# A vision-tower kernel on one Trainium2 core: variance of the last two images from row sums and squares, and the last attention, turns, counts and placings in another order

## What is computed

```python
h = tok_ref(x, scharr)                       # grey image, 2 edge filters, |.|, summed, /2
h = layernorm(h + attn(h, Wq, bq, Wk, bk, Wv, bv))
h = layernorm(h + ffn(h, Wr, W1, W2))

def layernorm(x, eps=1e-5):
    return (x - mean(x)) / sqrt(var(x) + eps)

# ffn: each token goes to its best expert, if it is among that expert's first 320
probs = softmax(t @ Wr); idx = argmax(probs); pmax = max(probs)
pos   = position of the token among those of its expert (a running count)
ein   = tokens of each expert; h = relu(ein @ W1); eout = h @ W2
out   = where(pos < 320, eout * pmax, t)
```

## Time and profile before

| | |
|---|---|
| median of 3 runs | 245.89 us (245.63 to 246.35) |
| the profiled execution | 245.8 us, of it a span of 244.1 us in the trace |
| PE busy | 230.0 us, 94% |
| DVE busy | 185.3 us, 76% |
| ACT busy | 152.2 us, 62% |
| POOL busy | 96.6 us, 40% |
| stage one, stretch between, stage two | to about 100 us, 100 to 110.5 us, 110.5 to 234.7 us (last matmul), then the last rows |

### The profile page before, as it was taken

How to read it: one execution, slowest core, us unless ns; L and a number is a source line. 1 busy time by engine, 2 the same in 40 slices (tenths; PEclk the granted TensorE clock), 3 DMA queues, 4 the chain that set the end, 5 groups by cost and what they waited for, 6 DMA issues and landing times.

```text
span 244.1 us, 5000 instructions
## 1 busy us (share of the span) xinstructions
PE 230.0 (94%) x1670; PEld 222.3 (91%) x1670; DVE 185.3 (76%) x558; ACT 152.2 (62%) x355; POOL 96.6 (40%) x170
## 2 busy tenths in 40 slices
PE   6999999999999999889999999999999999999940
PEld 5999999999999998658999999999999999999940
DVE  6878797787979798897676767967779677789550
ACT  5336567786877887466675676674766757666100
POOL 7001228474665656557000025232262322623672
PEclk9999999999999999999999999999999999999995
DMA  5925975083796020301899919064090650100100
GB/s 169 299 74 178 284 234 151 26 237 151 238 394 228 6 83 3 85 0 50 245 352 361 349 48 359 3 214 167 12 379 10 201 176 3 48 0 24 36 4 0
DMA packets 28666, 35.88 MB, mean 147 GB/s; under 512 B 2684, under 2 KB 25579, under 8 KB 28642
## 3 DMA queue, kind: packets, MB, share of 16 engines
q1 hardware_dynamic: 26434, 32.11, 40.8%
q0 software_dynamic: 1792, 3.47, 3.9%
q10 hardware_dynamic: 416, 0.00, 0.1%
HBM read 27.37 MB, written 9.47 MB: 151 GB/s over the span
## 4 chain that ended last, share of the span: by engine, by line
PE 85%; issue 4%; POOL 4%; DVE 3%; ACT 2%; POOLq 1%; DMA 0%; ACTq 0%; DVEq 0%
PE bank L1329 16%; PE bank L1330 15%; PE bank L1331 15%; PE bank L1400 14%; PE bank L1417 5%; PE bank L1454 5%; POOL out_dram L589 3%; PE bank L1586 2%; PE bank L1470 2%; PE bank L1636 2%; PE bank L1494 2%; PE bank L1428 2%; PE bank L1472 1%; PE bank L1471 1%; POOL yrstd L613 1%
## 5 line engine op out<-in xcount | busy, mean ns | idle before, releaser
L1243 DVE SCALAR_TENSOR_TENSOR h_lo<-bank,h_hi 128x320 fp32r<-128x320 f32 x58 | 28.3, 490 | 24.7 <-ACT h_hi L854 21.9
L854 ACT ACTIVATE h_hi<-bank 128x320 fp32r<-128x320 f32 x58 | 25.4, 438 | 34.6 <-PE bank L1331 34.6
L1329 PE MATMUL bank<-einT_hi,w_hi 128*128 128x320 f32 x128 | 40.3, 315 | 0.2 <-DVE einT_lo L1235 0.2
L1331 PE MATMUL bank<-einT_hi,w_lo 128*128 128x320 f32 x128 | 39.6, 309 | 0.0
L1330 PE MATMUL bank<-einT_lo,w_hi 128*128 128x320 f32 x128 | 39.5, 309 | 0.0
L589 POOL DMA_INDIRECT out_dram<-tokens_mem,images x24 | 27.7, 1155 | 29.3 <-ACT tokens_mem L871 22.2
L992 DVE TENSOR_TENSOR w_lo<-w_raw,w_hi 128x1024 fp32r<-128x1024 f32 x32 | 38.9, 1216 | 0.0
L1329 PE MATMUL bank<-h_hi,w_hi 128*128 128x320 f32 x112 | 35.1, 313 | 0.0
L1330 PE MATMUL bank<-h_lo,w_hi 128*128 128x320 f32 x112 | 34.6, 309 | 0.0
L1331 PE MATMUL bank<-h_hi,w_lo 128*128 128x320 f32 x112 | 34.6, 309 | 0.0
L771 ACT ACTIVATE w_hi<-w_raw 128x1024 fp32r<-128x1024 f32 x32 | 33.7, 1054 | 0.0
(11 more groups left out here) (235 smaller groups left out, 570.9 us busy)
## 6 DMA issues: line engine op xcount, KB each, us to landing
w_raw<-in_L_ffn_W_dram SPq DMA_DIRECT2D x16, 1024.0 KB, 8.0
images<-in_x_dram SPq DMA_DIRECT2D x7, 768.0 KB, 5.1
dispatched<-blank SPq DMA_DIRECT2D x4, 645.0 KB, 9.6
images<-dispatched SPq DMA_DIRECT2D x6, 387.0 KB, 9.2
out_dram<-lone SPq DMA_DIRECT2D x8, 256.0 KB, 7.7
images<-dispatched SPq DMA_DIRECT2D x3, 258.0 KB, 4.4
images<-in_x_dram SPq DMA_DIRECT2D x2, 384.0 KB, 5.3
out_dram<-tokens_mem,images POOLq DMA_INDIRECT x24, 3.5
```

Source lines behind the costliest of these rows:

```text
L854: act.activation(hidden_halves(n)[0], hidden_bank(n)[:, 0:CAP], ACT.Relu).then_inc(h_hi_ready, 1)
L1243: dve.scalar_tensor_tensor(lo, hidden_bank(n)[:, 0:CAP], 0.0, hi.bitcast(F32), ALU.max, ALU.subtract).then_inc(h_ready, 1)
L1329: pe.matmul(to, ah, bh, start=first, stop=False)
L1331: return pe.matmul(to, al, bh, start=False, stop=last)
```

## The change

For images 6 and 7 (L - 1 and L) the statistics are no longer made by bn_stats and bn_aggr. The residual sum on DVE also gives the row's sum (`accum_out`), DVE makes the negative mean of it (`row_mean`), ACT squares the residual with that as its bias and sums it (`square_rows`), and POOL makes variance, epsilon and power. The rows of image 6 are normalised by DVE (`norm_late_rows`) rather than by ACT; of image 7 the lower half is normalised by ACT (`norm_last_rows`) and the upper half by DVE.

The lists of the stretch are reordered. On PE `keep_warm(4)` is gone; `early_turn` is cut in two, one part for each chunk, and the first part stands between `late_prob_t` and `late_attend`, the second between the turn of the upper block and its product; the lower half's two products are swapped; three placings of image 6 stand ahead of `count(7)` and one behind; image 7 is placed with the lower half first. On DVE the bias of the upper half comes after `compare(6)`, the reciprocals, the gate sums and the means are cut by halves and stand beside the half that they belong to, and `number(6)` comes before the residual. On ACT the squares of image 6 stand before the first probabilities, `late_values(0)` after `late_prob_t`. `lsub` has two buffers.

```diff
@@ vector: the list of the last two images @@
             keys_low(L)
+            row_mean(L - 1, slice(0, SC), SC * L)
             residual_in(L, 0)
             residual_in(L, 1)
             softmax_max(L)
-            moments(L - 1)
             compare(L - 1)
-            softmax_sum(L)
+            late_bias(1, 0)
+            late_sum(0, 1)
+            for s in range(SC):
+                norm_late_rows(L - 1, s, L)
             add_places(L - 1)
-            late_residual()
-            moments(L)
+            number(L - 1)
+            late_residual(0, 1)
+            late_gate(1)
+            row_mean(L, slice(1, 2), SC * L + 1)
+            late_sum(1, 0)
+            late_residual(1, 0)
+            late_gate(0)
+            row_mean(L, slice(0, 1), SC * L + 2)
             route(L)
             factor(L - 1)
-            number(L - 1)
             compare(L)
+            norm_late_rows(L, 0, L + SC)
             add_places(L)
@@ vector: new functions @@
+            def row_mean(b, s, residuals):
+                dve.wait_ge(resid_ready, residuals)
+                dve.tensor_scalar(row_nmean[:, b % 2, s], row_sum[:, b % 2, s], -1.0 / D, None, ALU.mult
+                                  ).then_inc(row_mean_ready, 1)
+            def norm_late_rows(b, s, scales):
+                dve.wait_ge(rstd_ready, scales)
+                dve.wait_ge(rows_out[b % TR], 16 * SC * (b // TR))
+                dve.tensor_scalar(trow[:, b % TR, s, 0:D], resid[:, b % 2, s, :], row_nmean[:, b % 2, s:s + 1],
+                                  rstd[:, b % 2, s:s + 1], ALU.add, ALU.mult).then_inc(late_t_ready, 1)
@@ scalar @@
+            def square_rows(b, s, means):
+                act.wait_ge(pT_done, b + 1)
+                act.wait_ge(row_mean_ready, means)
+                act.activation(prob[:, s, :], resid[:, b % 2, s, :], ACT.Square, bias=row_nmean[:, b % 2, s:s + 1],
+                               accum_out=row_square[:, b % 2, s:s + 1]).then_inc(row_square_ready, 1)
...
             late_values(1)
+            for s in range(SC):
+                square_rows(L - 1, s, 1)
+            act.wait_ge(row_square_ready, SC)
+            late_probs(0, 1)
             late_constant(0)
-            late_probs(0, 1)
+            late_prob_t()
             late_values(0)
-            late_prob_t()
             late_probs(1, 0)
             late_prob_t_top()
-            norm_rows(L - 1)
             route_exp(L - 1)
-            norm_rows(L)
+            square_rows(L, 1, 2)
+            square_rows(L, 0, 3)
+            norm_last_rows()
             route_exp(L)
@@ gpsimd @@
+            def scale_square(b, s, squares):
+                pool.wait_ge(row_square_ready, squares)
+                link(pool.tensor_scalar(ve[:, s], row_square[:, b % 2, s], 1.0 / D, EPS, ALU.mult, ALU.add))
+            def scale_last_rows():
+                b = L
...
+                for n, s in enumerate((slice(1, 2), slice(0, 1))):
+                    scale_square(b, s, SC + n + 1)
+                    ins = pool.tensor_tensor(rstd[:, b % 2, s], ve[:, s], minus_half[:, s], ALU.pow)
+                    if n == 0:
+                        link(ins)
+                        ins = pool.tensor_tensor(nmr[:, b % 2, s], row_nmean[:, b % 2, s], rstd[:, b % 2, s], ALU.mult)
+                    ins.then_inc(rstd_ready, 1)
@@ tensor @@
-            keep_warm(4)
...
+            def early_turn(c):
+                pe.wait_ge(rowc_ready, L + SC - c)
+                pe.wait_ge(late_values_ready, SC - c)
                 pe.wait_ge(ein_in[0], 32)
                 pe.wait_ge(spare_rows_ready, 1)
...
-            early_turn()
-            place(L - 1)
+            late_prob_t()
+            early_turn(1)
+            late_attend()
+            late_prob_t_top()
+            early_turn(0)
+            late_attend_top()
+            place(L - 1, 1, 0)
+            place(L - 1, 1, 1)
+            place(L - 1, 0, 0)
             count(L)
-            place(L)
+            place(L - 1, 0, 1)
+            for c in range(DC):
+                for s in (1, 0):
+                    place(L, c, s)
```

More of the change, by code:

```diff
@@ L743, in norm_lone @@
                 act.wait_ge(lone_scale_ready, b + 1)
[L744 removed]
+                act.wait_ge(t_ready, SC * (b + 1) if b < L - 1 else SC * (L - 1) + (b - L + 1))
+                if b >= L - 1:
+                    act.wait_ge(late_t_ready, SC + b - L + 1)
                 if b >= 2:
@@ L759, in route_exp @@
                 for s in range(SC):
-                    ins = act.activation(lexp[:, s, :], lsub[:, s, :], ACT.Exp, scale=rstd[:, b % 2, s:s + 1],
+                    ins = act.activation(lexp[:, s, :], lsub[:, b % 2, s, :], ACT.Exp, scale=rstd[:, b % 2, s:s + 1],
                                          accum_out=lsum[:, s:s + 1])
@@ L1127, in compare @@
                 if b >= L - 1:
-                    for s in range(SC):
+                    for s in range(SC) if b < L else (1, 0):
                         dve.tensor_scalar(pick(b, s), slot_index, mine[:, b % 2, s, 0:1], None, ALU.is_equal
@@ L1548, in late_attend @@
                           ).then_inc(attn_done, 1)
-            late_prob_t()
-            late_attend()
-            def place(b):
-                for c in range(DC):
-                    for s in range(SC):
-                        pe.wait_ge(pick_ready, SC * (b - L + 1) + s + 1)
-                        pe.wait_ge(t_ready, SC * b + s + 1)
-                        ins = pe.matmul(bank[c][:, 0:CAP], trow[:, b % TR, s, c * P:(c + 1) * P], pick(b, s),
-                                        start=False, stop=(b == L and s == SC - 1),
-                                        skip_group_check=True)
-                    if b == L:
-                        ins.then_inc(einT_done, 1)
@@ L1565, in early_turn @@
-            def early_turn():
-                pe.wait_ge(rowc_ready, B + 1)
-                pe.wait_ge(late_values_ready, SC)
+            def early_turn(c):
+                pe.wait_ge(rowc_ready, L + SC - c)
+                pe.wait_ge(late_values_ready, SC - c)
                 pe.wait_ge(ein_in[0], 32)
                 pe.wait_ge(spare_rows_ready, 1)
-                for c in range(DC):
-                    for j, (o, _) in enumerate(SLOTS):
-                        ins = pe.matmul(bank[c][:, o:o + P], ein[:, 0, j, c * P:(c + 1) * P], ident[:, :],
-                                        start=(j == 0), stop=False, is_transpose=True, skip_group_check=True)
+                for j, (o, _) in enumerate(SLOTS):
+                    ins = pe.matmul(bank[c][:, o:o + P], ein[:, 0, j, c * P:(c + 1) * P], ident[:, :],
+                                    start=(j == 0), stop=False, is_transpose=True, skip_group_check=True)
@@ L1574, in early_turn, with place @@
                 ins.then_inc(early_turned, 1)
-            early_turn()
-            place(L - 1)
+            def place(b, c, s):
+                if b < L:
+                    pe.wait_ge(pick_ready, s + 1)
+                    pe.wait_ge(late_t_ready, s + 1)
+                elif s == 1:
+                    pe.wait_ge(pick_ready, SC + 1)
+                    pe.wait_ge(t_ready, SC * (L - 1) + 1)
+                else:
+                    pe.wait_ge(pick_ready, SC + 2)
+                    pe.wait_ge(late_t_ready, SC + 1)
+                last = b == L and s == 0
+                ins = pe.matmul(bank[c][:, 0:CAP], trow[:, b % TR, s, c * P:(c + 1) * P], pick(b, s),
+                                start=False, stop=last, skip_group_check=True)
+                if last:
+                    ins.then_inc(einT_done, 1)
```

124 lines of the change are left out of this document (81 added, 43 removed).

## The result

The changed kernel takes 251.04 us (250.52 to 251.29, 6 runs), the kernel before 246.53 us (245.63 to 246.89, 6 runs) beside it: a ratio of 1.0187, 95% interval 1.0169 to 1.0204, +4.5 us. The prediction was 247.1 us, 246.3 to 249.0. The sign was right; the change costs nearly four times what was forecast, and the time lies outside the range.

A forecast was written before the change was run, and what follows sets the result against it. PE, busy 94%, bounds the kernel; the change can only move its first expert matmul. 1.98 - 1.07 + 0.35 = 1.26, less 0.05 for rounding, gives +1.2 us on a median of 245.89: 247.1 us, range 246.3 to 249.0.

The forecast's parts named there:

- PE held by the load: At the first part of early_turn, PE waits for expert 0's rows until about 103.2; +0.75 to +1.8 us, chance 0.60.
- late start: Behind PE's wait for expert 0's rows, the upper residual comes at 106.06 instead of 104.08, 1.98 us later.
- Statistics off DVE's path: On DVE from upper residual to onehot, bn_stats, bn_aggr, epsilon and one gate sum are gone; -1.07 us.
- Normalisation on DVE: norm_late_rows(7, 0) joins DVE's list behind the picks, lengthening the way from onehot to split by 0.35 us.
- Square needs no other table: ACT's squares need no table switch; the rival, another function table, was +1.5 us, 248.6 us, chance 0.05.
- Variance and power: On POOL for image 7, they end at 108.65 while DVE is busy until 109.0, so their wait costs nothing.
- The clock, rival at 0.15: PE falls to the lower clock with filler gone and wait in; +1.2 to +3.2 us, about 249.3 us, chance 0.15.
- the fillers' removal: On PE, the four filler matmuls ended before the turns they preceded; removal gives at most 0.2 us, hidden.
- Load of expert 1: Scatters of images 6 and 7 and this load go 0.8 us later, its PE user 1.2; listed as costing nothing.

The follow-up runs named there:

- b_turn_early: The kernel before with the first part of early_turn ahead of late_attend, filler matmuls kept; 249.4 us, ratio 1.0145.
- a_fill: The changed kernel with 4 filler matmuls at their old place and 8 more between late_prob_t and the first part of early_turn; 249.5 us.
- b_no_fill: The kernel before without its four filler matmuls, keep_warm(4); 246.38 us, ratio 1.0015.
- a_turn_late: The changed kernel with both parts of early_turn put back behind the last attention; 246.63 us, ratio 1.0018.
- ein6: a_turn_late with expert 1's turn (PE, ACT and DVE) one hidden tile later in expert 0; 246.56 us, ratio 1.0033.
- split: a_turn_late with the DVE weight split that follows einT_lo moved behind the first hidden tile; 246.08 us, ratio 1.0004.
- a_fill4: The changed kernel with only the four filler matmuls back in their old place; 249.16 us, ratio 1.0115.
- a_nudge: a_turn_late with the four fillers back and a DVE memset of 320 columns ahead of split_low(2); 246.47 us, ratio 1.0017.
- a_small4: a_turn_late with the four fillers back and four DVE reciprocals of 128x2 ahead of split_low(2); 245.72 us, ratio 0.9977.

## Why the prediction was wrong

- *PE held by the load*: right. Expected turn at about 103.45, landing 103.24 plus 0.2. The trace of after starts 0.41 later, the load's second piece was issued at 101.06, and the turn is at 103.89, 0.23 behind a landing 2.6 us after the issue. From the upper residual to the first expert matmul it is 5.76 us (108.49 to 114.25) where the forecast had 5.7. Price of the late start 1.98 predicted, 2.12 in b_turn_early.
- *Statistics off DVE's path, -1.07*: residual to onehot went from 2.65 to 1.47 us (108.49 to 109.96), -1.18. Right.
- *Normalisation on DVE, +0.35*: from onehot to the first expert matmul was 3.82 and is 4.12 us in a_fill, +0.30. Right, and it stands right behind the picks, without idle.
- *Square needs no other table*: right, there is one table load in the trace of after as well. Variance and power were not waited for.
- *The clock, rival at 0.15*: this is the step that failed. The mechanism and its price were on record (+1.2 to +3.2; measured +2.1), but the forecast took it not to happen, since the one fall in the trace of before came about 3.9 us after work had stopped and "the transposes in the gap speak against". One reading at the end of the span bounded nothing: over the sixteen traces the fall there came 2.3 to 5.1 us after the last matmul. Here the clock fell at 102.6, 2.2 us after the last matmul of `count(6)` had ended (100.4), with only two short transposes between; in all six runs the clock was down. With the fillers' removal listed as hidden ("at most 0.2 us"), I costed what the fillers take and not what they do. Their worth is in the odds: with `early_turn` in its late place, 9 of 44 runs without them had the clock down (b_no_fill, a_turn_late, ein6, split), and none of 72 with them. The two groups did not run on the same chips. Beside the 44, on their chips, the kernel before with its fillers had it down in 1 of 42 (248.34 us, the only one of its 114 runs near 246 us; three more of 330 to 802 us are out of line with everything else and left out), which speaks against the chip as the reason.
- *Load of expert 1, "whose user on PE moves by 1.2 us"*: this step failed too, for 0.8 us; the forecast put its wait at nothing. I moved the scatters by 0.8 us and gave all a constant length. They went out from 112.28 in place of 108.18, the third took 1.92 in place of 0.98, the last landing took 3.4 in place of 2.3 us, and the load left at 120.60 in place of 114.83. Its user had moved 3.7. Even with the clock held it is late (1.7 us in a_fill). DVE's list had been shifted against POOL's by a few tenths, and I had not looked at what runs beside a scatter.

Sum, on the profiled execution: 1.17 (as forecast, on the stretch) + 2.12 (clock) + 0.8 (expert 1's load) is 4.1 of the 4.7 us by which the span grew; 0.4 is the start of the run and 0.2 lies in stage two. The medians differ by 4.5.

The clock alone does not explain the miss. With the clock held, a_fill takes 249.5 us and three runs of a_fill4 take 248.75 to 249.53, near the top of the range (249.0) or above it; the traces of the two kernels show a wait for expert 1's load of 1.7 and 1.6 us, with three of the four scatters held. Since all six runs of the changed kernel had the clock down, its own time with the clock held was not measured; 246.53 + 1.17 + 0.8 to 1.7 + 0.2 gives an estimate of 248.7 to 249.6. So the forecast of the stretch was right for its reasons, and it takes both failed steps to get to the 4.5.

Left open: what decides in a given run whether the clock falls. Idle time of PE makes it likelier, but the same program goes both ways, and in a_turn_late_ein6 it fell with no idle time above 0.67 us. Open too are why a last scatter lands late, and the 0.5 us of PE in ein6 without a releaser.

## What to carry to other kernels

A wait of two microseconds on TensorE has two prices, its length and the odds of the lower clock behind it, here 1.4 to 2.1 us more; put a turn or any small consumer of a load behind work that does not need it, and treat fillers as insurance whose removal shows only in some runs. When a list on VectorE or GpSimd moves, look at what the two now do at the same time: 0.15 us of order between a large VectorE instruction and a scatter decided about 0.9 us of a scatter. Take many runs of kernels near such an edge, since one trace may show either case.

## What the hardware showed unexpectedly

*A scatter waits for a large VectorE instruction.* Over the sixteen traces, each scatter of GpSimd that started while a split of 128 x 1024 (1.2 us, both inputs in SBUF) ran ended 0.78 to 0.96 us after the split's end and took never less than its plain 0.97 us; these are 112 cases:

| split began before the scatter by | scatter takes |
|---|---|
| 1.05 to 1.20 us | 0.97 to 1.00 us |
| 0.76 to 0.77 us | 1.28 to 1.30 us |
| 0.41 to 0.46 us | 1.57 to 1.66 us |
| 0.27 to 0.29 us | 1.71 to 1.79 us |
| 0.14 to 0.16 us | 1.90 to 1.92 us |
| 0.04 to 0.12 us | 2.03 to 2.04 us |
| begins 0.10 us or more after it | 0.97 to 1.09 us (a_nudge apart) |

Most of the cases are in stage two, once for each of five experts (1.57 to 1.75 us); in before PE never waits there for it. A subtraction with one input in PSUM (`einT_lo`) that runs when a scatter starts does not delay it (0.98 us for the scatter at 111.15 in before, beside an `einT_lo` from 110.88 to 111.37). The memset of a_nudge fits the rule if it holds the scatter too; that is one case, with small instructions in its place as the only cross-check.

The Trainium skill (SBUF — State Buffer, "Who interferes with whom") says that VectorE and GpSimd share a pair of ports under an exclusive lock, and that a VectorE instruction with two inputs in SBUF holds up a GpSimd instruction that reads SBUF; the table agrees with that. The same section infers that such an instruction does not hold up the making of descriptors for a DMA; the scatters of these traces end 0.78 to 0.96 us after it, which speaks against the inference. It also says that a VectorE instruction with at most one input in SBUF does not contend with GpSimd outside two-port modes, against which the one case of the memset, with no input, may stand.

*The clock.* In the changed kernel it fell when PE had had nothing but two short transposes for 2.2 us. At the end of the span it fell 3.9 us after the last matmul in before, and between 2.3 (a_small4) and 5.1 us (b_turn_early) over all traces. In a_turn_late_ein6 it fell although PE had not been idle for more than 0.67 us at a time since `count(6)`. In the changed kernel it stayed down from 102.6 to 109.4 although PE was busy again from 103.9. The products of 264 columns cost 1.09 in place of 0.61 us meanwhile.
